# A decoder layer on one core: another order of work at its begin, its seam and the ends of its feed-forward

## The reference, cut to what matters

```
x = x + attn(layernorm(x))                    # linear attention with rotated q, k; causal mask, no softmax
x = x + xattn(layernorm(x), context)          # 16 heads of 32, softmax(q k / sqrt(32) + bias) v, 224 x 750
x = x + ffn(layernorm(x))                     # gate, up and down, 512 -> 2048 -> 512, weights rounded to -1, 0, 1,
                                              # activations rounded to 8 bits by row
```

## Time and profile before

| | us |
|---|---|
| median of 3 runs | 1225.41 (1221.86 to 1235.33) |
| the profiled execution | 1222.01, its span 1220.4 |
| TensorE busy | 1165.0 (95% of the span) |
| VectorE, ScalarE, GpSimd busy | 811.7, 590.3, 540.3 |
| granted TensorE clock, mean | 0.991 of full speed |

### The profile page before, as it was taken

How to read it: one execution, slowest core, us unless ns; L and a number is a source line. 1 busy time by engine, 2 the same in 40 slices (tenths; PEclk the granted TensorE clock), 3 DMA queues, 4 the chain that set the end, 5 groups by cost and what they waited for, 6 DMA issues and landing times.

```text
span 1220.4 us, 25146 instructions
## 1 busy us (share of the span) xinstructions
PE 1165.0 (95%) x9483; PEld 898.7 (74%) x9483; DVE 811.7 (67%) x1494; ACT 590.3 (48%) x967; POOL 540.3 (44%) x443
## 2 busy tenths in 40 slices
PE   5899999998889999999999999999999988899996
PEld 5788888886768778887878878778788766454443
DVE  7677666667456666566665666666665588688883
ACT  4223222335245445445444444454444577588785
POOL 5021111116035666665675675765666231333240
PEclk9999999999999999999999999999999999999999
DMA  6222322425624344344343343352442685122121
GB/s 194 83 84 88 128 81 93 140 82 181 157 59 113 74 109 116 82 126 110 78 133 99 78 136 82 88 154 54 110 130 52 182 251 157 54 65 69 60 69 44
DMA packets 75252, 129.45 MB, mean 106 GB/s; under 512 B 18353, under 2 KB 34869, under 8 KB 75140
## 3 DMA queue, kind: packets, MB, share of 16 engines
q1 hardware_dynamic: 62747, 104.28, 30.9%
q0 software_dynamic: 12416, 23.96, 6.0%
HBM read 68.96 MB, written 11.22 MB: 66 GB/s over the span
## 4 chain that ended last, share of the span: by engine, by line
PE 82%; DVE 9%; ACT 2%; issue 2%; DMA 2%; SPq 1%; POOL 1%; DVEq 0%; ACTq 0%; POOLq 0%
PE xa_psR L2010 27%; PE sa_psR L61 14%; PE xa_psO L2067 7%; PE xa_psM L2043 7%; PE xa_psS L2024 6%; PE xa_psM L1186 4%; PE xa_psO L1204 4%; PE sa_psE L753 4%; DVE xa_m_part L1828 2%; PE xa_psS L1186 2%; DVE sa_et L509 1%; PE sa_psO L770 1%; PE xa_psO L2077 1%; DMA cv<-in_ctx_dram 1%; PE xa_psR L1195 1%
## 5 line engine op out<-in xcount | busy, mean ns | idle before, releaser
L1828 DVE TENSOR_REDUCE xa_m_part<-xa_psM 112x1 f32<-112x376 f32 x512 | 266.6, 545 | 222.6 <-PE xa_psM L2043 220.0
L1732 ACT ACTIVATE space<-xa_psS 125x448 f32<-125x448 f32 x384 | 208.6, 545 | 173.0 <-PE xa_psS L2024 171.2
L1593 POOL TENSOR_TENSOR xa_sum_space<-xa_sum_space,space 125x896 f32<-125x896 f32 x112 | 237.8, 2123 | 97.5 <-ACT space L1732 93.1
L2043 PE MATMUL xa_psM<-xa_k,xa_q 104*112 104x376 f32 x512 | 160.7, 352 | 7.2 <-DMA xa_q<-xa_q_st 2.9
L2024 PE MATMUL xa_psS<-xa_q,xa_k 104*125 104x224 f32 x768 | 146.1, 272 | 2.4 <-ACT space L1732 2.4
L2024 PEld LDWEIGHTS xa_psS<-xa_q,xa_k 104*125 104x125 f32 x768 | 137.7, 188 | 5.7 <-ACT space L1732 3.6
L2043 PEld LDWEIGHTS xa_psM<-xa_k,xa_q 104*112 104x112 f32 x512 | 87.3, 175 | 27.4 <-DVE xa_m_part L1828 9.9
L2067 PE MATMUL xa_psO<-space,cv 125*32 125x224 f32 x1536 | 94.8, 359 | 0.9 <-ACT space L1732 0.9
L1576 POOL TENSOR_SCALAR xa_oT_hi<-xa_o_f 128x224 fp32r<-128x224 f32 x32 | 25.4, 792 | 152.7 <-DVE xa_o_f L1844 152.7
L2010 PE MATMUL xa_psR<-xa_cT_hi,w_lo 128*128 128x376 f32 x256 | 91.2, 356 | 0.0
L2010 PE MATMUL xa_psR<-xa_cT_lo,w_hi 128*128 128x376 f32 x256 | 86.7, 339 | 0.0
(11 more groups left out here) (219 smaller groups left out, 2665.4 us busy)
## 6 DMA issues: line engine op xcount, KB each, us to landing
xa_k<-xa_k_st SPq DMA_DIRECT2D x378, 94.0 KB, 2.2
xa_q<-xa_q_st SPq DMA_DIRECT2D x192, 56.0 KB, 2.0
cv<-in_L_ffn_w_gate_dram SPq DMA_DIRECT2D x14, 512.0 KB, 4.9
cv<-in_ctx_dram POOLq DMA_DIRECT2D x7, 1000.0 KB, 12.0
cv<-in_L_ffn_w_down_dram SPq DMA_DIRECT2D x10, 512.0 KB, 7.1
cv<-in_L_ffn_w_up_dram SPq DMA_DIRECT2D x9, 512.0 KB, 6.0
sa_x_raw<-in_x_dram SPq DMA_DIRECT2D x8, 448.0 KB, 7.4
sa_rows<-in_x_dram SPq DMA_DIRECT2D x8, 448.0 KB, 3.8
```

The costliest lines, as they stand in the source:

```text
L1593: nc.gpsimd.tensor_tensor(p_sum[:], before, tile, ALU.add).then_inc(p_summed, 1)
L1732: nc.scalar.activation(pT[:, (s + i) % 2, j], psS[0:KB, (HG * i + j) % EXP_BANKS, 0:2 * N], ACT.Exp).then_inc(exp_done, 1)
L1828: V.tensor_reduce(m_part[:, t, jj, seg:seg + 1], psM[0:T, seg, 0:SEG], AX.X, ALU.max).then_inc(mx_read, 1)
L2043: M.matmul(psM[0:T, seg, 0:SEG], q4[0:ROWS, g, jj, t * T:(t + 1) * T], k4[0:ROWS, g % 2, jj, seg * SEG:(seg + 1) * SEG], start=True, stop= ...
```

## The change

The order of work is changed in eight places, and one subtraction moves from VectorE to GpSimd, two roundings and a copy from ScalarE to VectorE.

```
 # begin: SyncE
             load_weight(1)
+            sp.wait_ge(w_in[0], DMA)
             sp.dma_start(g1_raw[:], ...)            # then g2_raw, four times
 # begin: VectorE
-            make_angles()
+            place_positions()                       # the first copy of make_angles, on its own
             statistics(0)
             mean_and_variance(0)
+            make_angles()
             make_turns()
 # seam: SyncE
             load_weight_ahead(3)
+            pack_keys(0, 0)
             load_x(1)
-            pack_keys(0, 0)
 # seam: GpSimd
             pool.wait_ge(sa.stored, DMA * B)
+            pool.wait_ge(q_packed[0], QPACK)
             load_context(1, 0)
+            pool.wait_ge(w_split_hi, 2)
+            nc.gpsimd.tensor_tensor(w_lo[:, 3], w_raw[:, 1], w_hi[:, 3].bitcast(F32), ALU.subtract).then_inc(w_split_lo, 1)
+            load_context(1, 1)
...
-                    if s == 0 and b + 1 < B:
+                    if s == 0 and 0 < b < B - 1:
                         load_context(b + 1, 1)
 # seam: VectorE, at the takes of K0a, q0, q1
                     normalise(0)
+                if what == "q0":
                     sa_centre(B - 1)
-                if what == "q0":
+                if what == "q1":
                     sa_finish(B - 1)
...
                 reduce_half(0, half)
-                if half == 3:
-                    split_weight(3)
 # ScalarE
             def exponentials(b, s, i, j):
+                if (n, i, j) == (0, 0, 0):
+                    act.wait_ge(w_split_lo, 2)
 # the value tile V5 goes into the first slot, beats 6 to 8
-    first_values = ["V2", "V3", "V4", "V5"]
+    first_values = ["V2", "V3", "V4"]
+    LATE_VALUES = {(0, 0): {6: ("V5", 0)}}
...                                                  # fillers() merges it in; TensorE's attend() waits for
                                                     # the two value tiles of each part, no more for all six
 # feed-forward, ScalarE's body(i)
-            for half in range(2):
-                round_hidden(i, half)
-            silu(i + 1, 0)
+            round_hidden(i, 0)
+            if is_first(i):
+                silu(i + 1, 0)
+            round_hidden(i, 1)
+            if not is_first(i):
+                silu(i + 1, 0)
 # and body(0) is taken out of the loop, on ScalarE and TensorE
-            with act.Fori(0, TILES - 2) as i:
+            body(0, True)
+            with act.Fori(1, TILES - 2) as i:
 # feed-forward, TensorE's body(i)
             for c in range(3):
                 gate_up(i + 1, c)
+            if is_first(i):
+                for full_read, count in places["outputs_read"]:
+                    pe.wait_ge(full_read, count)
             turn_hidden(i, 0)
...                                                  # the same wait is gone ahead of the loop
 # feed-forward, last tile: ScalarE's end
             for half in range(2):
                 round_hidden(TILES - 1, half)
-            for half in range(2):
-                finish_hidden(TILES - 1, half)
-            for half in range(2):
-                copy_turned_h(TILES - 1, half)
+            copy_turned_h(TILES - 1, 0)
 # and VectorE's
+        def finish_hidden(i, half):
+            dve.wait_ge(hm_ready, 2 * i + half + 1)
+            wait_count(dve, h_turned, 2 * i)
+            cs = slice(half * NC // 2, (half + 1) * NC // 2)
+            V.tensor_scalar(hq[:, cs], hm[:, cs], MAGIC, QMAX, ALU.subtract, ALU.min).then_inc(hq_ready, 1)
+
+        def copy_second_half(i):
+            dve.wait_ge(h_turned, 2 * i + 2)
+            dve.wait_ge(hq_T_ready, 2 * i + 1)
+            V.tensor_copy(hq_T[:, HALF:].rearrange("p k c -> p (k c)"), psT[1]).then_inc(hq_T_ready, 1)
...
             down_dequantiser(TILES - 1)
+            for half in range(2):
+                finish_hidden(TILES - 1, half)
+            copy_second_half(TILES - 1)
             add_residual(TILES - 1)
```

More of the change, by code:

```diff
@@ L558, in vector, with place_positions, make_angles @@
             middle = round((two_pi - high) * 2 ** 20) / 2 ** 20
-            def make_angles():
+            def place_positions():
                 dve.wait_ge(const_made, 5)
                 V.tensor_copy(pos[:], pos_i[:]).then_inc(table_step, 1)
+            def make_angles():
                 dve.wait_ge(table_step, 2)
@@ L1222, in rest @@
             turn_x(1)
-            for full_read, count in places["outputs_read"]:
-                pe.wait_ge(full_read, count)
-            with pe.Fori(0, TILES - 2) as i:
+            body(0, True)
+            with pe.Fori(1, TILES - 2) as i:
                 body(i, True)
@@ L1317, in fillers @@
     def fillers(b, s):
-        return {k: (what, batch_of(what, b)) for k, what in (fill if b < B - 1 else last_fill)[s].items() if 0 <= batch_of(what, b) < B}
+        parts = {k: (what, batch_of(what, b)) for k, what in (fill if b < B - 1 else last_fill)[s].items() if 0 <= batch_of(what, b) < B}
+        return dict(sorted((parts | LATE_VALUES.get((b, s), {})).items()))
     def part_at(b, s, k):
@@ L2058, in attend @@
                     pe.wait_ge(w_scale_step, 1) if n == 0 else pe.wait_ge(o_ready, n)
-                    for t in range(NK) if s == 0 else ():
-                        pe.wait_ge(read[bank_of[f"V{t}", b]], use_of[f"V{t}", b])
+                for t in (2 * i, 2 * i + 1) if s == 0 else ():
+                    pe.wait_ge(read[bank_of[f"V{t}", b]], use_of[f"V{t}", b])
                 for a in range(2):
@@ L2108, in _ @@
                 maxima_half(0, half)
-                if half < 12:
+                if half < 3 * len(first_values):
                     do(first_values[half // 3], 0, half % 3)
```

## The result

Over 14 runs each the changed kernel took 1216.76 us (1214.91 to 1223.44), the kernel before 1225.81 (1221.86 to 1235.33); the ratio is 0.9936, 95% interval 0.9919 to 0.9954. The profiled execution has a span of 1214.9 us against 1220.4, mean granted clock 0.992 against 0.991. The two medians are 9.05 apart; the spans of the two profiled executions only 5.5. The difference comes from the kernel before, whose median lies 3.8 above its profiled run (1222.01), while the changed kernel's lies at its own (1216.84); what those other runs of before lose has no profile and stays open.

What follows compares the result with a forecast made beforehand. TensorE was taken as busy nearly throughout, with waits at the begin, the seam and the feed-forward's ends. Terms of 0.5 + 4.3 + 1.9 + 0.3 + 0.7 - 0.9 + 1.1 + 1.0 = 8.9 off 1222.0 gave 1213.1; median 1214.5, range 1211 to 1217.5.

Steps and rivals of the forecast that it cites:

- Begin: Kernel start, 0 to 15 us: angles behind x(0)'s statistics, G1 and G2 held until Wq lands; 0.5 us gained.
- Seam: Between self-attention and cross-attention: earlier K0 packs and faster landing of queries start the first maximum 4.3 us sooner.
- Just covered: In the seam: x(1), loaded behind K0's packs, lands at 314.6, before TensorE ends K1a at about 315.
- Maxima: First maxima: three more halves without a value tile part gain 1.9 us, the subtraction moved to GpSimd 0.3.
- Context's stall: Second slot: context(1)'s second part goes out earlier, so TensorE's 0.70 wait at 378.44 goes; 0.7 us gained.
- V5: First slot: value tile V5's three parts, moved there to beats 6 to 8, cost 0.9 us.
- Feed-forward's begin: First tile: the wait for both outputs moves behind three products and silu goes between two roundings; 1.1 us gained.
- Feed-forward's end: Last tile: ScalarE's two last roundings and a copy go to VectorE, so the down product starts 1.0 us sooner.
- 1.4 for runs that spread upward: Whole kernel: the median was put at 1214.5, 1.4 above the sum's 1213.1, because runs spread upward only.
- case of 1228: Slower rival: the clock falls in the bare first maxima and stays down, kernel ends at 1228; chance 0.03.
- x(1) takes context's place: Seam rival: x(1)'s load moves among the queries' packs, first maximum 2.9 us later than forecast, 1217.4; chance 0.25.
- The clock stays up: Rival: shorter gaps spare low clock behind the first maxima and in two feed-forward products; 4.2 more, 1210.3; chance 0.13.

Runs made afterwards that it cites:

- two clean profiles: Profiles of the changed kernel with its begin undone, 1217.55 us, and with x(1)'s load ahead of K0's packs and GpSimd's subtraction waiting for VectorE's three-column instruction, 1214.02 us.
- guarded kernels: Changed kernel with x(1)'s load ahead of K0's packs and GpSimd's subtraction waiting for VectorE's three-column instruction, 1214.02 us; the same with V5 back among the first maxima, 1214.85 us.
- guarded kernel: Changed kernel with x(1)'s load ahead of K0's packs and GpSimd's subtraction waiting until VectorE's three-column instruction has ended: 1214.02 us.
- changed kernel's second profile: Profile from running the changed kernel again with nothing changed, beside three later variants: 1218.45 us over six runs.
- x(1) first alone: Changed kernel with the load of x(1) put back ahead of the packs of K0, nothing else changed: 1215.14 us.

## Why the prediction was right

The median, 1216.76, lies 2.3 above the 1214.5 predicted, inside the range. The mechanisms of the seam, of context's stall and of the feed-forward came as described; the begin did not. By its own steps, in the first profile and then in ones that no stretch or collision touches:

- **Begin, 0.5 predicted, 0 measured.** Wq lands at 9.99, not sooner than 9.94. I took the middle of the bounds on the ground of G1's packets; the lower bound was right. The wait on SyncE cost nothing either: Wv's copy starts at 19.50, where 19.65 was the limit.
- **Seam, 4.3 predicted, 3.6 measured** (29.60 to 26.03), and 4.3 to 4.7 in the profiles at 24.95 to 25.27. Start of the packs (301.6 predicted, 301.79) and landing (2.0, 1.97) are as forecast. The missing 0.7 is SyncE's issue of x(1), which took 1.55 there, where I had counted 0.4; over the profiles with it behind K0's packs it took 0.43 to 1.82. "Just covered" was wrong, x(1) landing 3.4 later than I had it, but TensorE's slack ahead of the queries absorbed it. That slack was luck. I had TensorE ready at 321.3 with the clock as low as before; from its first product for q0 it took 18.47 in the kernel before, with the 6.8 us at 1.2 GHz, and 16.43 to 16.46 in the changed profiles without the stall. By these rows (an estimate) the stalled TensorE would have been ready 2.0 later, at 323.9, 1.8 behind the landing of the queries, had the clock fallen there again.
- **Maxima, 2.2 predicted, 0.5 measured** (16.42 to 15.94). In the two clean profiles it is 2.0 (14.40), of which 0.40 is the subtraction (predicted 0.3). The rest of the 2.2 went to the clock: 0.57 over 322 to 326, with a product of 512 columns every 0.43 us instead of 0.23.
- **Context's stall, 0.7 predicted, 0.66 measured**, the same in all thirteen profiles with the edit.
- **V5, -0.9 predicted, -1.1 measured**, 1.18 between the guarded kernels.
- **Feed-forward's begin, 1.1 predicted, 2.33 measured.** The two waits gave 0.88 and 0.27, as worked out; the third product's 1.3 I had put into a rival, and it came every time. Of the steps that repeat in every profile this is the one that was mis-sized most; in the first profile alone the maxima's 1.7 is more, and that was the clock.
- **Feed-forward's end, 1.0 predicted, 0.98 measured.** The last product runs at either level, 4.99 or 3.71: 9 of the 12 profiles with the edit have the short one and neither of the two without it, so 1.3 more comes often, though not in the profile shown.

The measured terms sum to 3.41 + 0.48 - 1.09 + 0.66 + 2.33 + 0.98 = 6.8, the begin's loss of 0.16 being in the first; a stretch at 1.2 GHz at 998, which the profile before has not, takes 1.0 back (from the third turn to the first anchor of the feed-forward it is 665.7 against 664.7), and what is left agrees with 5.5 to 0.3. The prediction's sum of 8.9 is 2.1 above: begin, seam and maxima 3.1 too high in this profile, V5 0.2 and the feed-forward 1.2 too low in size. The medians' 9.05 is nearer to it because the kernel before has its median 3.8 above its profiled run (1222.0); the sum was one of profiled runs, and its closeness to 9.05 is luck. The forecast itself was saved by part of its 1.4 for runs that spread upward: the changed kernel's median lies at its profiled run, so the 1.4 was not needed and took up 1.4 of the 3.7 by which 1213.1 was too low. One bound was also misread: by the 12.3 us that the prediction takes for a change, its case of 1228 would not have been slower.

Of the rivals, "x(1) takes context's place" was right in kind and fell in size. x(1) took 7.5 itself, and the twelve queries' packs landed a median of 3.7 behind their issues, against 2.4 in the guarded kernel; but the last of them, which decides, landed after 1.97. In four of the eight profiles with x(1) behind K0's packs it took 2.5 to 2.6, so 0.6 of the rival's 2.9 comes at times. The slower case fell, though the sign that the prediction gave for being wrong, more than 4 us at 0.50 behind the maxima, came in the changed kernel's second profile (6.8 from 342.7) and in seven of the variants'; no stretch outlasted 7 us. "The clock stays up" was right for the product at 1054, right in 9 of 12 for the last one though not in the first profile, wrong behind the turn. What no rival held was the collision. The prediction asked of the subtraction on GpSimd only who waits for it, not which VectorE instructions run beside it.

Open: how often the collision comes over the changed kernel's 20 runs; half of them lie above 1218 and the guarded kernel's highest of six is 1217.74, which fits, but only two of the 20 have a profile.

The guarded kernel, 1214.02 us, beats both: 4.4 below the changed one on the same chip (the intervals of their ratios, 0.9874 to 0.9919 and 0.9900 to 0.9943, overlap by little), 12.7 below the one before. That this is the guard's doing is not shown; x(1) first alone gave 1215.14, in another set of runs.

## What to carry to other kernels

When an elementwise operation moves to GpSimd, list every VectorE instruction that may run beside it or beside GpSimd's DMA issues, the smallest too, and order GpSimd's work behind those that read and write SBUF. Here a 4.5 us stall came by chance, and no profile has it in which x(1)'s load came first and VectorE's small instruction ended ahead of GpSimd's issue; the smallest of those margins was 0.30, so the order should be made by a wait and not left to the times. When a wait disappears and the time stays, look at the queue that feeds the next wait: SyncE's 24 packs, some 0.63 to 0.72 us each, bounded the seam whatever VectorE did. Compare distances between anchors and count the time at 1.2 GHz before believing the difference of two spans.

## What was not expected of the hardware

A `tensor_scalar` of 128x3 lasted 5.57 us beside GpSimd's DMA issue and subtraction, and 0.14 alone. The issue alone is enough to hold one: a normalising pair took 1.64 instead of 1.00 beside it. It holds the other way round too: GpSimd's power of 112x2 took 3.27 in the changed kernel, beside VectorE's 128x2048 subtraction (3.26 or 3.27 in all thirteen profiles with the changed seam), and 1.06 before. The same DMA issue on SyncE (x(1), 448 KB) took between 0.34 and 1.82. And the clock of the product at 1054 went with the waits ahead of it: with a wait of 1.99 behind one of 1.92 it ran at 1.2 GHz in two of two profiles, with 1.72 behind 1.04 at 2.4 GHz in twelve of twelve.
